# One batch's projection, feed-forward and q, k, v moved among the attention windows of the layer before, and causal lead-in jobs moved into its last window

## The reference

```
x = x + attn_a(layernorm(x))      # 16 heads of 8, all keys
x = x + ffn(layernorm(x))         # (silu(n Wg^T) * (n Wu^T)) Wd^T, hidden 384, weights int * 1/127
x = x + attn_b(layernorm(x))      # 16 heads of 8, causal
x = x + ffn(layernorm(x))

attn(n): q, k, v = n Wqkv + b
         softmax(q k^T / sqrt(8)) v, heads joined, Wout + bout
```

## Time and profile before

| | |
|---|---|
| median of 3 runs | 1333.21 us (1331.50 to 1336.69) |
| the profiled execution | 1338.29 us, span 1336.4 us |
| PE busy | 1290.7 us, 97% |
| DVE busy | 1176.7 us, 88% |
| ACT busy | 1004.5 us, 75% |
| POOL busy | 142.1 us, 11% |
| chain that ended last | PE 88%, DVE 5%, ACT 3% |
| granted TensorE clock, mean | 0.968 |

### The profile page before, as it was taken

How to read it: one execution, slowest core, us unless ns; L and a number is a source line. 1 busy time by engine, 2 the same in 40 slices (tenths; PEclk the granted TensorE clock), 3 DMA queues, 4 the chain that set the end, 5 groups by cost and what they waited for, 6 DMA issues and landing times.

```text
span 1336.4 us, 26857 instructions
## 1 busy us (share of the span) xinstructions
PE 1290.7 (97%) x9681; PEld 656.2 (49%) x9681; DVE 1176.7 (88%) x2979; ACT 1004.5 (75%) x1791; POOL 142.1 (11%) x309
## 2 busy tenths in 40 slices
PE   8899999999999999999988987999999999999998
PEld 6434343433434443434335764555555555555487
DVE  7699999999999999999926988799899999999276
ACT  8678888888888888888884531677777777777753
POOL 5630000000000000000002211200000000000011
PEclk9689999999999999999999996799999999999999
DMA  7611001111101111100000433112111211120001
GB/s 209 204 33 34 21 14 34 33 33 34 32 8 29 34 33 33 33 23 13 2 1 1 122 99 95 34 39 59 36 35 38 59 37 34 35 64 4 3 25 40
DMA packets 40060, 58.44 MB, mean 44 GB/s; under 512 B 7796, under 2 KB 19448, under 8 KB 39928
## 3 DMA queue, kind: packets, MB, share of 16 engines
q1 hardware_dynamic: 39928, 56.72, 17.7%
HBM read 36.77 MB, written 18.87 MB: 42 GB/s over the span
## 4 chain that ended last, share of the span: by engine, by line
PE 88%; DVE 5%; ACT 3%; issue 2%; DMA 1%; SPq 0%; POOL 0%; DVEq 0%; ACTq 0%; POOLq 0%
PE psum L1166 30%; PE psum L1132 21%; PE psum L1100 21%; PE psum L1253 4%; PE psum L1028 3%; PE psum L1237 2%; ACT probs L653 2%; PE psum L1140 2%; PE psum L1039 1%; DVE maxima L882 1%; DVE hid L958 1%; PE psum L1182 1%; PE psum L1077 1%; PE psum L1013 1%; PE psum L1150 1%
## 5 line engine op out<-in xcount | busy, mean ns | idle before, releaser
L653 ACT ACTIVATE probs<-psum 128x512 f32<-128x512 f32 (+3 forms) x1386 | 821.8, 669 | 153.0 <-PE psum L1132 83.0
L882 DVE TENSOR_REDUCE maxima<-psum 128x1 f32<-128x512 f32 x1232 | 767.8, 682 | 8.6 <-PE psum L1100 6.6
L1100 PE MATMUL psum<-kop,qop 62*128 62x512 f32 (+2 forms) x1744 | 519.4, 429 | 7.0 <-DVE maxima L879 3.1
L1132 PE MATMUL psum<-qop,kop 64*128 64x512 f32 (+3 forms) x1792 | 514.2, 427 | 9.2 <-ACT probs L653 7.9
L1166 PE MATMUL psum<-probs,v 128*32 128x512 f32 (+3 forms) x3584 | 440.5, 564 | 0.7 <-ACT sums L660 0.7
L1100 PEld LDWEIGHTS psum<-kop,qop 62*128 62x128 f32 x1744 | 266.4, 189 | 203.4 <-DVE maxima L882 119.3
L1132 PEld LDWEIGHTS psum<-qop,kop 64*128 64x128 f32 x1792 | 247.5, 187 | 232.1 <-ACT probs L653 205.9
L879 DVE CUSTOM_DVE_ANT_0 junk<-psum,mask 128x512 bf16<-128x512 f32 (+3 forms) x512 | 232.6, 487 | 38.7 <-PE psum L1100 34.9
L1166 PEld LDWEIGHTS psum<-probs,v 128*32 128x32 f32 x3584 | 71.1, 108 | 120.0 <-issue 89.2
L546 POOL TENSOR_TENSOR att<-att_raw,rden 128x128 f32<-128x128 f32 x64 | 26.1, 409 | 536.9 <-DVE rden L911 536.9
L1140 PE MATMUL psum<-half_ident,key_mask 64*128 64x64 bf16 x1024 | 74.3, 197 | 0.0
(11 more groups left out here) (102 smaller groups left out, 750.4 us busy)
## 6 DMA issues: line engine op xcount, KB each, us to landing
qop<-q_parts SPq DMA_DIRECT2D x256, 64.0 KB
kop<-k_parts SPq DMA_DIRECT2D x64, 128.0 KB
kop<-k_parts SPq DMA_DIRECT2D x128, 64.0 KB
q_parts<-parts SPq DMA_DIRECT2D x24, 256.0 KB, 2.9
k_parts<-parts SPq DMA_DIRECT2D x24, 256.0 KB, 3.2
x<-in_L_attn_a_x SPq DMA_DIRECT2D x8, 256.0 KB, 4.6
q_parts<-att SPq DMA_DIRECT2D x8, 256.0 KB, 3.7
k_parts<-att SPq DMA_DIRECT2D x8, 256.0 KB, 3.8
```

The lines of the kernel that those rows point to most:

```text
L653: nc.scalar.activation(probs[:, slot, heads[0] % 2:heads[-1] % 2 + 1, c0:], psum[:, bank:bank + len(heads), c0:], ACT.Exp, scale=SCORE_SCA ...
L882: nc.vector.tensor_reduce(dst, src, AX_X, ALU.max).then_inc(ring_free, 1)
L1100: mm(psum[:, bank, 0:width], qop[rows, buf, f, r, qb * P:(qb + 1) * P].bitcast(F32R), kop[rows, buf, r, kh * CHUNK:kh * CHUNK + width].bit ...
L1132: ins = mm(psum[:, bank + k, c0:], kop[rows, buf, c // 2, j * P:(j + 1) * P].bitcast(F32R), qop[rows, buf, f, c // 2, c0:].bitcast(F32R), ...
```

## The change

`spread_chunk` gives the places of one chunk's pieces in the walk: (window, step) and what stands there after the step's last unit. Chunk 0 is spread over windows 4 to 7, chunk 1 over 8 to 11. Pieces of three kinds exist. Those in `UNIT_KINDS` take a bank of the unit ring: transposes of the heads, of the normalised rows and of the new rows, the three gates, q and k. Those in `JOB_KINDS` take a bank of the job ring: projection, three ups, `down`, v. `gather`, `moments` and `normalise` are steps on ScalarE, VectorE and GpSimd without a bank. Normalisation moves to ScalarE for these chunks (scale and bias per row, the bias from GpSimd's new `negative_centre`), and the two subtractions of low parts to GpSimd (`low_rows`, `low_parts`). The stage between handles chunks 2 to 7 (`SPREAD = 2`), and the early chunk of the last window is chunk 2.

The 59 causal lead-in jobs (`LEAD`) stand in the last window and just behind it, wherever a `j` has no job of the first layer left. The shift of causal window 0, half 0, follows as `causal_shift`. The operands of causal windows 0 and 1 are loaded in turn with the first layer's, that of window 2 with `causal_shift`. The two-head units of the last window (`wide_step`) are gone, and so are the causal jobs inside the stage.

```diff
+                    if w >= WINDOWS and followed < follow:
+                        self.walk.append(("causal_job", None, followed, None))
+                        followed += 1
...
-                    if w == WINDOWS - 1 and x[0] >= wide_step:
-                        if x[1][0] % 2 == 1:
-                            continue
-                        x = x[0], (x[1][0], x[1][0] + 1)
-                        self.wide_from = min(self.wide_from, taken)
...
+                        for piece, chunk, part in (spread or {}).get((w, x[0]), ()) if x[1][-1] == HG - 1 else ():
+                            if piece in UNIT_KINDS:
+                                self.walk.append((piece, chunk, taken, part))
+                                taken += 1
+                            elif piece in JOB_KINDS:
+                                self.walk.append((piece, chunk, jobs, part))
+                                jobs += 1
+                            else:
+                                self.walk.append((piece, chunk, None, part))
...
+UNIT_KINDS, JOB_KINDS = ("heads", "rows", "gate", "new", "qk"), ("project", "up", "down", "v")
+SPREAD = 2
...
+def spread_chunk(n, w):
...
+    return {(w, 1): [("gather", n, None)], (w, 4): [("heads", n, None)], (w, 7): [("project", n, None)],
+            (w, 9): [("moments", n, 1)], (w, 13): [("normalise", n, 1)],
+            (w + 1, 1): [("rows", n, None)], (w + 1, 6): [("gate", n, c) for c in range(FB)],
+            (w + 1, 9): [("up", n, 0)], (w + 1, 11): [("up", n, 1)], (w + 1, 13): [("up", n, 2)],
+            (w + 2, 1): [("down", n, None)], (w + 2, 3): [("moments", n, 0)], (w + 2, 8): [("normalise", n, 0)],
+            (w + 2, 12): [("new", n, None)],
+            (w + 3, 1): [("qk", n, 0)], (w + 3, 2): [("qk", n, 1)], (w + 3, 6): [("v", n, None)]}
...
-              jobs_ahead=48, sums_behind=2, project_at=(9, 11, 14), wide_step=5),
+              jobs_ahead=48, sums_behind=2, project_at=(9, 11, 14),
+              spread={**spread_chunk(0, 4), **spread_chunk(1, 8)}, follow=LEAD),
...
+                    if kind == "causal_shift":
+                        wait(sp, sums_done, WINDOWS * plan.n)
+                        load_operands(2, (WINDOWS + 2) % BUFS)
+                        shift_to_operand(f, (WINDOWS + w) % BUFS, PLANS[0].units_all + number)
...
-            for m in range(-1, CHUNKS + (layer == 0)):
-                body(m, *(n if first <= n < CHUNKS else None for n, first in
+            begin = SPREAD if layer == 0 else 0
+            for m in range(begin - 1, CHUNKS + (layer == 0)):
+                body(m, *(n if begin + first <= n < CHUNKS else None for n, first in
...
+                    elif kind == "gate":
+                        nc.scalar.activation(hid[:, part, :], src, ACT.Silu, scale=DEQUANT).then_inc(probs_ready, 1)
...
-                wait(pe, ring_free, job_base + number - plan.job_ring + 1)
+                wait(pe, ring_free, job_base + max(number - plan.job_ring + 1, 0) if layer else number - plan.job_ring + 1)
...
+                        if banks[3] == banks[2]:
+                            pe.wait_ge(ffn_low_ready, layer * CHUNKS + n + 1)
...
+                    elif kind == "down":
+                        pe.wait_ge(ring_free, copied["gated"])
+                        for t in range(TPC):
+                            ins = down_products(t, bank)
...
-                        if layer == 1 and number == 0:
-                            pe.wait_ge(qk_ready, 4 * CHUNKS)
-                            pe.wait_ge(v_ready, 2 * CHUNKS)
+                        if layer == 1 and number == 1:
+                            pe.wait_ge(qk_ready, 2 * (2 * CHUNKS - SPREAD))
+                            pe.wait_ge(v_ready, 2 * CHUNKS - SPREAD)
```

439 lines of the change are left out of this document (286 added, 153 removed).

## The result

The changed kernel takes 1366.49 us (median of 4 runs, 1365.10 to 1367.33), the kernel before beside it 1332.67 (1331.50 to 1336.69). The ratio is 1.024, 95% interval 1.022 to 1.026. The forecast was 1301 with a range of 1288 to 1317, so the time lies 65 us above the one and outside the other.

What follows compares the result with a forecast made beforehand. VectorE was taken to bound the first layer's attention, TensorE a close second. Terms -22.2 - 30.6 + 19.4 + 1 + 0 = -32.4 us took the profiled 1338.29 to 1305.9, less 5.1 for the median: 1301 us, range 1288 to 1317.

Steps and rivals of the forecast that it cites:

- TensorE is a close second ... some 3 us of 39.4 are free: First-layer attention window: sums, products and transposes take TensorE 36.4 us of 39.4, leaving some 3 us free.
- over four windows it has about 4 x 3 us free ... so on the average it fits: Windows with pieces: a chunk's TensorE work, at most 11.1 us, fits the free time plus 6.4 us that VectorE adds.
- two chunks among the windows: Windows 4 to 11: inserting two chunks costs 9.7 us each, +19.4 us together, bounds 12.8 and 27.
- the 13.5 that I had as the upper bound: Per chunk in the windows: without TensorE slack, its 11.1 us and 2.4 us blocked by table switches are all paid.
- So VectorE sets the pace and whatever goes onto it there is paid in full.: First-layer windows: VectorE's row maxima take 39.2 of 39.4 us, so added VectorE work, 6.4 us per chunk, costs its length.
- The two subtractions went to GpSimd, the two normalisations to ScalarE, which have room.: Windows with pieces: these steps were left out of the 6.4 us per chunk counted for VectorE.
- `down` is one burst of 2.84 us: Windows with pieces: `down` fills a job slot, at most three maxima stay outstanding, so VectorE idles about 1 us.
- rival (3): Windows: each of 28 inserted pieces drains the job ring, 2.4 us each, giving 1361 us; chance 0.04.
- The end of the first layer (+1): Last window to last reciprocal: 59 causal lead jobs there, with 6 us for waits, add 1 us; bounds -4 and +6.
- Two turns less: Stage between the layers: batch 0's two chunks leave it, saving two turns of 11.10 us, -22.2 us.
- The lead-in leaves the seam: From the last `down` to the first causal scores: 59 causal jobs no longer stand there, -30.6 us.
- (1): Windows 4 to 11: TensorE becomes the bound and switches block, two chunks cost 27 us, giving 1312 us; chance 0.18.

Runs made afterwards that it cites:

- b1: Kernel before, plus two more sets of four 128x128 transposes on TensorE at each of the first layer's 32 half ends; 1358.69 us, ratio 1.019.
- c1: Changed kernel with seven edits where TensorE's queue stood still, in the windows with pieces and the last window, including those of t1 and w1; 1331.72 us, ratio 0.998.
- b2: Kernel before, plus two more 128x512 passes on VectorE at each of the first layer's 32 half ends; 1346.44 us, ratio 1.009.
- b3: Kernel before, plus two more 128x512 copies on ScalarE at each of the first layer's 32 half ends; 1366.13 us, ratio 1.024.
- c5: Changed kernel with only c1's last-window edits: ring wait, normalise on GpSimd, heads turned a step later, causal shift split first; 1350.39 us, ratio 1.011.
- t1: Changed kernel with the job ring's ordinary wait instead of waiting for all first-layer jobs before the first causal lead-in job; 1359.08 us, ratio 1.018.
- t2: Changed kernel with seven small matrix products filling TensorE's wait before the first causal lead-in job; 1359.13 us, ratio 1.018.
- c3: c1, but GpSimd no longer waits for all v before it splits the second causal shift; 1329.92 us, ratio 0.996.
- w1: Changed kernel with each spread chunk's second moments moved from behind head group 3 to behind head group 5; 1355.33 us, ratio 1.015.
- w2: Changed kernel with the spread chunks' SiLU computed as a scaled Exp, so ScalarE loads no other table there; 1359.55 us, ratio 1.019.
- c2: Changed kernel with only c1's edits in windows with pieces: second moments later, normalise on GpSimd, q and k's cast and low part behind the shift; 1341.78 us, ratio 1.005.
- c4: c3, plus one tiny Exp on ScalarE behind the last q and k to load the table early; 1332.96 us, ratio 0.997.

## Why the prediction was wrong, step by step

**The step that failed is "TensorE is a close second ... some 3 us of 39.4 are free", and with it "over four windows it has about 4 x 3 us free ... so on the average it fits".** I built TensorE's budget from 0.15 us per product, read where it issued without a wait, and set this sum above the row that said 20.00 busy in 20. The sum used the shortest spacing for all products, while at the ends of the halves ScalarE's exponentials set the pace; b1 put 1.7 us per window there and paid 1.6. Hence the term "two chunks among the windows" was not 9.7 but 29.8 per chunk. Of chunk 0's, 9.6 came back with other queues and places (2.8, 3.4, 1.8 and 1.6 in its four windows); about 20 stay with every piece in place (c1; 19 in chunk 1 with no half clock at all), against the 13.5 that I had as the upper bound. That bound took a turn of 11.1 for TensorE's whole work and found nothing lost around it; in the trace the pieces' products alone are 3.9 for gates and up, 2.9 for `down`, 2.3 and 1.2 for q, k and v, 1.2 for the projection and some 2 of transposes, 13.5, and TensorE's busy time rises by about 15 (after) to 16 us (c1), clock taken out.

**"So VectorE sets the pace and whatever goes onto it there is paid in full."** This failed too, in the harmless direction: b2 put 1.67 us per window on VectorE and paid 0.85, and with the pieces in place it is TensorE that sets the pace, while VectorE is idle for 22.7 of 187.6 us. (The four parts of the 6.4 us add up to 6.5; that changes nothing.)

**"The two subtractions went to GpSimd, the two normalisations to ScalarE, which have room."** Room in the mean, not in place. ScalarE's lumps are paid at three quarters (b3), and GpSimd, busy for 11% of the span, held TensorE for 2.97 us by its order alone. I had asked what each engine does, not what stands behind it in its queue.

**"`down` is one burst of 2.84 us"** stood right (2.94 at 322.94), and so did the 1.28 of the table loads and that the gates cost about 1.5 us of stop: 1.41. What I left out was the clock. I priced it only at the seam, and named half clock in the windows as a sign of rival (3) alone.

**"The end of the first layer (+1)".** The sum without waits gave 704.5; with nearly all stops gone (c5) the end still takes 42.1 us from the shift, which is 713.9 on the clock of before, 9 us later than the 704.7 I had for TensorE. In these 42.1 us it is busy for 39.5, where I had 33.2 us of work, and idle for 2.7. The 6 us for waits were then 12.6 (54.7 less 42.1), and 6.0 to 6.6 of them came with a single wait, the one for the drained ring, and the clock behind it (t1, t2). I had named this very wait and the shared bank, but not what TensorE does after standing still.

**"Two turns less" (-22.2)** was right: -21.6, the turn stays at 11.10. **"The lead-in leaves the seam" (-30.6)** was right in kind and came at -26.4. The last q, k and v ran at 1.2 GHz (3.75 and 1.74 us where 1.88 and 1.05 were counted, 2.6 us), the bound of +3 that I had named. Of the rest 0.9 is GpSimd's shift: 1.13 us at 867.12 instead of 0.22, behind a wait for v that it did not need (c3). Behind the first causal scores the kernel is 4.5 us shorter, where I counted 0 for the clock and allowed 6: half clock lasts for about 7 us there, for about 17 before.

Of the rivals, (1) named the right engine and (3) the right symptom, half clock; neither had the size. The two chunks cost 60 us, more than twice the 27 of (1), and only (3)'s time, 1361, was close. That is luck: TensorE stands still for over half a us at four places of a chunk, not at each of its 14 pieces. It had a chance of 0.04, though its break-even of 1.4 us per piece lay well within reach: 59.7 less my floor of 12.8 is 1.7 us for each of the 28 pieces, all causes together. The sign of the change hung on that one figure, and I had fixed it by an average.

Settled by runs: the clock's part at the end of the layer (t1, t2), the stops in the windows (w1, w2, c1, c2), that TensorE has no slack at a half end, and ScalarE's price there (b1, b3). Not tested apart: how the 20 us per chunk that remain in c1 divide into the pieces' own products (13.5 by the trace) and a loss around each; b1 to b3 only show that a lump at a half end is paid at nine tenths of its length on TensorE, three quarters on ScalarE and half on VectorE. Whether the clock stays up behind a given wait is open as well.

## What to carry to other kernels

A sum of the shortest spacings is not a budget, and neither is the row of busy time: TensorE and VectorE both stood at 99% or more of these windows, and a lump cost nine tenths of its length on one and half on the other. Before a change whose sign hangs on such a slack, put a lump of the same size on the engine, at the place, and measure it; b1 is three lines. In a loop that passes each tile through three engines with two or three banks between them, an engine that is idle an eighth of the time may have little room for a lump (here three quarters of it were paid): ask what stands behind the lump in its queue and who waits for that, on GpSimd as well. And TensorE's waits are to be priced with the clock behind them: here 1.4 us of standing still cost 6 us in some executions and almost nothing in others, and 34 us came back by moving work between queues and hardly removing any.

## What was not expected of the hardware

- A wait of TensorE as short as 0.64 us (380.02) stood ahead of a stretch at 0.64 of the clock, and one of 1.43 us ahead of some 12 us at half clock, which was absent where seven small products filled the wait (t2). It isn't a fixed rule: c2_win kept 2.4 GHz behind the like of the second, b3 had 23 waits of up to 0.6 us with the clock at 1.00, and c3 and c4 have the same two waits (2.24 and 0.77 us) in front of the last q, k products, and these took 1.96 us in c3 and 3.35 in c4.

```profile
826.67 1.96 PE L1197 MATMUL psum<-xt,wqkv 128*128 128x512 f32 x4 [0.77 <-ACT xt L703]
```

```profile
829.14 3.35 PE L1201 MATMUL psum<-xt,wqkv 128*128 128x512 f32 x4 [0.77 <-ACT xt L704]
```

  Such a difference may be part of why these kernels scatter by 0.5% and more: c4 goes from 1327.65 us at a mean clock of 0.983 to 1335.96 at 0.976.
- GpSimd's shift of 128x16, 0.22 us in the windows, took 1.25 us where VectorE had begun a subtraction with two inputs in SBUF 0.05 us earlier (c1_all, VectorE's row and then GpSimd's); both end at about the same time. In the changed kernel it took 1.13 us at 867.12, 0.16 us behind the start of the same subtraction.

```profile
829.53 1.23 DVE L944 TENSOR_TENSOR parts<-qk,parts 128x1024 f32<-128x1024 f32 x1
```

```profile
829.58 1.25 POOL L602 TENSOR_TENSOR shift<-negmax,zeros 128x16 bf16<-128x16 f32 x1 [6.49 <-DVE v L935]
```

  The Trainium skill ("SBUF — State Buffer", section "Terms") says that VectorE and GpSimd share one pair of ports under a lock held for the whole instruction; these two rows agree.
